# Feed-forward gate product: the second gate goes through a bfloat16 tile in SBUF

## The reference, cut to what matters

```python
def _qdot(x, w, out_dtype=BF16):
    return jnp.dot(x.astype(E4M3), w.astype(E4M3), preferred_element_type=out_dtype)
ff_gate = _qdot(x, w_gating[0])        # 512 -> 2048
gate_value = jax.nn.gelu(ff_gate)
ff1 = _qdot(x, w_gating[1])            # the second gate
activations = gate_value * ff1         # rounded to E4M3 by the next _qdot
outputs = _qdot(activations, w_linear) # 2048 -> 512
```

## Time and profile before

| what | us |
|---|---|
| median of three runs | 1949.02 |
| the profiled execution's own time | 1948.51 |
| its span | 1946.7 |
| TensorE busy in the span | 1867.8 (96%) |
| VectorE busy | 1484.0 (76%) |
| ScalarE busy | 1116.2 (57%) |
| GpSimd busy | 989.0 (51%) |
| first and last product (start) | 1582.5 and 1925.3 |

### The profile page before, as it was taken

The page is one execution under the profiler, slowest core; times in us unless marked ns, Lnnn a source line. Parts: engine busy times, 40 slices in busy tenths (PEclk is TensorE's granted clock), DMA queues, the critical chain, the costliest instruction groups (busy, mean ns, idle before and its releaser), DMA issues.

```text
span 1946.7 us, 31849 instructions
## 1 busy us (share of the span) xinstructions
PE 1867.8 (96%) x11426; PEld 1052.8 (54%) x11460; DVE 1484.0 (76%) x2632; ACT 1116.2 (57%) x2149; POOL 989.0 (51%) x1000
## 2 busy tenths in 40 slices
PE   7899999999999898899999999999999898999998
PEld 4677776777777654344444444444444333444443
DVE  4557676675666657788888888888888548999998
ACT  3345443444444525788888888888888662333331
POOL 3455545555455522344555455444444246666665
PEclk9999999999999878999999999999999999999999
DMA  5665554655555522334433333333333320111111
GB/s 170 177 160 151 134 162 120 175 138 149 147 141 145 140 81 74 110 106 135 135 130 119 114 114 118 122 121 122 121 117 100 116 71 12 44 44 44 46 63 44
DMA packets 149901, 220.58 MB, mean 113 GB/s; under 512 B 41847, under 2 KB 50551, under 8 KB 148999
## 3 DMA queue, kind: packets, MB, share of 16 engines
q1 hardware_dynamic: 140078, 216.96, 37.1%
q10 hardware_dynamic: 9664, 1.58, 0.5%
HBM read 83.95 MB, written 32.02 MB: 60 GB/s over the span
## 4 chain that ended last, share of the span: by engine, by line
PE 73%; DVE 14%; DMA 4%; POOL 3%; ACT 3%; issue 3%; SPq 1%; ACTq 0%; DVEq 0%; POOLq 0%
PE bank L1298 12%; PE bank L1333 11%; PE bank L85 8%; PE bank L1631 7%; PE bank L86 7%; PE bank L87 7%; PE bank L1341 6%; PE bank L1607 4%; PE bank L577 4%; DVE sa_mneg L703 3%; PE bank L631 3%; DVE sa_xnat L717 2%; PE bank L644 2%; DVE ff_prod L1648 1%; DVE ff_hq L1662 1%
## 5 line engine op out<-in xcount | busy, mean ns | idle before, releaser
L1376 DVE TENSOR_REDUCE xa_mneg<-bank 128x1 f32<-128x512 f32 x1024 | 641.9, 681 | 114.7 <-PE bank L1341 109.9
L1196 ACT ACTIVATE xa_prob<-bank 128x512 f32<-128x512 f32 x1024 | 545.1, 609 | 80.6 <-PE bank L1333 77.7
L1341 PE MATMUL bank<-xa_kst,xa_qst 48*128 48x512 f32 x1024 | 383.1, 459 | 10.7 <-DVE xa_mneg L1376 10.6
L1333 PE MATMUL bank<-xa_qst,xa_kst 49*128 49x512 f32 x1024 | 354.2, 441 | 13.8 <-ACT xa_prob L1196 13.5
L468 ACT ACTIVATE sa_prob<-bank 128x512 f32<-128x512 f32 x256 | 152.4, 599 | 335.9 <-PE bank L631 334.9
L1333 PEld LDWEIGHTS bank<-xa_qst,xa_kst 49*128 49x128 f32 x1024 | 163.3, 186 | 295.6 <-ACT xa_prob L1196 241.7
L1298 PE MATMUL bank<-xa_prob,xa_v 128*32 128x512 f32 x2048 | 275.4, 610 | 0.0
L1539 POOL TENSOR_TENSOR ff_total<-ff_prod,ff_mag 128x512 f32<-128x512 bf16 x128 | 195.6, 1528 | 101.4 <-DVE ff_mag L1655 101.3
L703 DVE TENSOR_REDUCE sa_mneg<-bank 128x2 f32<-128x512 f32 x256 | 164.1, 683 | 35.7 <-PE bank L644 35.5
L1341 PEld LDWEIGHTS bank<-xa_kst,xa_qst 48*128 48x128 f32 x1024 | 166.1, 187 | 41.9 <-DVE xa_mneg L1376 34.0
L1583 ACT ACTIVATE ff_gelu<-bank 128x512 bf16<-128x512 f32 x128 | 75.6, 593 | 155.1 <-PE bank L1631 155.1
(11 more groups left out here) (191 smaller groups left out, 3663.5 us busy)
## 6 DMA issues: line engine op xcount, KB each, us to landing
xa_qst<-xa_part_q SPq DMA_DIRECT2D x192, 128.0 KB, 2.7
xa_kst<-xa_part_k SPq DMA_DIRECT2D x192, 128.0 KB, 2.8
sa_qst<-sa_part_qh SPq DMA_DIRECT2D x64, 256.0 KB, 4.1
sa_kst<-sa_part_kh SPq DMA_DIRECT2D x64, 256.0 KB, 5.4
xa_den<-inv SPq DMA_DIRECT2D x64, 256.0 KB
sa_xraw<-xT SPq DMA_DIRECT2D x32, 256.0 KB, 4.3
sa_qst<-sa_part_ql SPq DMA_DIRECT2D x32, 256.0 KB, 4.3
sa_kst<-sa_part_kl SPq DMA_DIRECT2D x32, 256.0 KB, 5.8
```

The costliest lines, as they stand in the source:

```text
L1196: act.activation(prob[place[e]][:, :], banks[eb[e]][:, :], ACT.Exp, scale=X_SCALE)\
L1333: pe.matmul(banks[eb[e]][:, :], kst[u % 3][rows_of, head // 2, t * P:(t + 1) * P], qst[u % 3][rows_of, head // 2, :], start=True, stop=Tru ...
L1341: pe.matmul(banks[mb[m]][:, :], qst[u % 3][rows_of, n // 8, t * P:(t + 1) * P], kst[u % 3][rows_of, n // 8, :], start=True, stop=True).the ...
L1376: dve.tensor_reduce(mneg[:, u % 2, column:column + 1], banks[mb[m]][:, :], AX.X, ALU.max, negate=True).then_inc(s_mfree, 1)
```

## The change

ScalarE copies the second gate of slot n from its PSUM bank into a new bf16 tile `up` in SBUF (three buffers, in the region "parts"), right behind the gelu of the same slot. The copy waits for the matmuls (`s_ub`) and for the product three slots back (`s_prod`). TensorE's reuse of an `ub` bank now waits for the copy (`s_up`), not for the product. VectorE's product waits for the copy and reads `up` and `gelu`, both bf16 in SBUF. The instructions of TensorE, GpSimd and the DMA queues are the same in number and order; ScalarE has 128 more.

```diff
+    up = r.sb("ff_up", [P, 3, COLS], BF16)
...
                 act.activation(gelu[:, n % 4, :], gb[n % 2][:, :], ACT.Gelu_apprx_tanh)\
                    .then_inc(s_gelu, 1)
+                wait.wait_ge(s_ub, n + 1)
+                wait.wait_ge(s_prod, n - 2)
+                act.activation(up[:, n % 3, :], ub[n % 2][:, :], ACT.Copy).then_inc(s_up, 1)
                 if p + 1 < PAIRS and h in turns:
                     round_x(p + 1, turns.index(h))
...
-                    for k, banks, done, free in [(0, gb, s_gb, s_gelu), (1, ub, s_ub, s_prod)]:
+                    for k, banks, done, free in [(0, gb, s_gb, s_gelu), (1, ub, s_ub, s_up)]:
...
             wait.wait_ge(s_gelu, n + 1)
-            wait.wait_ge(s_ub, n + 1)
+            wait.wait_ge(s_up, n + 1)
             wait.wait_ge(s_hs, n - 3)
-            dve.tensor_tensor(prod[:, n % 4, :], ub[n % 2][:, :], gelu[:, n % 4, :], ALU.mult)\
+            dve.tensor_tensor(prod[:, n % 4, :], up[:, n % 3, :], gelu[:, n % 4, :], ALU.mult)\
                .then_inc(s_prod, 1)
```

More of the change, by code:

```diff
@@ L1479, in ffn_phase @@
     s_tb, s_x8, s_xq = s.sem("tb"), s.sem("x8"), s.sem("xq")
-    s_gb, s_ub, s_gelu, s_prod = (s.sem(n) for n in ["gb", "ub", "gelu", "prod"])
+    s_gb, s_ub, s_gelu, s_up, s_prod = (s.sem(n) for n in ["gb", "ub", "gelu", "up", "prod"])
     s_he, s_hm, s_hs, s_hq = (s.sem(n) for n in ["he", "hm", "hs", "hq"])
```

## The result

| | before | after |
|---|---|---|
| median, us | 1949.02 (1944.70 to 1953.71, five runs) | 1965.18 (1963.69 to 1970.16, five runs) |
| ratio after / before | | 1.0089, 95% interval 1.0073 to 1.0106 |
| profiled execution, us | 1948.51 | 1963.69 |
| its span | 1946.7 | 1961.8 |
| start of the first product | 1582.5 | 1578.6 |

The kernel is slower, by 16.2 us of the medians; 1967 was forecast.

The account below looks back on a forecast made before the run. It took VectorE and TensorE to be both at their floor, so longer VectorE slots lengthen the kernel. Terms 7.0, 1.5, 8.9, 0.5 and 0 gave 17.9 us on 1948.5, 1966.4, so a median of 1967; range 1954 to 1985.

Parts of the forecast that it names:

- The product's own length: VectorE's product with both inputs bf16 in SBUF takes 0.42 us, 0.26 less than now.
- The hold and who goes first: In plain slots GpSimd's addition goes first and holds the product: 2.56 us instead of 2.09; other slots 2.89 and 3.16.
- Rival B: The product gets the port ahead of GpSimd's addition and the mask is held instead; 1958 us, chance 0.10.
- Pair 0: Pair 0 and the start of pair 1: 15 intervals at VectorE's pace, 0.47 us longer each, 7.0 us.
- The sets of four in pairs 1 to 7: Sets of four slots grow from 10.80 to 11.17 us, 0.37 each: 1.5 in rest of pair 1, 8.9 in pairs 2 to 7.
- The copies' latency: Where VectorE waits for the gelu, and in the first slot, copies add delay less the product's saving: 0.5 us in all.
- The tail: The 16 slots after the last product, all before the feed-forward, add 0.
- The signs: Plain-slot products about 1.4 us, ending 0.29 after GpSimd's addition, which stays 1.53; TensorE some 96% busy in the steady state.
- A: No hold on the product, or one that costs nothing; plain slots stay 2.09, TensorE's 10.75 stays; 1948 us, chance 0.11.
- C: The hold comes and the product stays at full length; plain slots 2.82, four slots 12.21; 2000 us, chance 0.09.
- D: Faster by over 0.3%: pair 1's two waits, 7.7 us, close as freed banks let TensorE run ahead; 1941, chance 0.03.
- S: Main rival in the experiments: loss comes from ScalarE's 128 copies, the wait for them and later freeing of banks.

Follow-up runs that it names:

- copies_only: Changed kernel with all 128 ScalarE copies kept and waited for, but the product reads the second gate from PSUM; 1951.47 us, ratio to before 1.0001.
- mixed: Changed kernel with copy and SBUF product only in 54 of 128 slots, behind the normalisation or statistics, PSUM in the others; 1946.56 us, ratio to before 0.9986.
- up_f32: Changed kernel with the tile `up` in float32 instead of bf16; 2002.74 us, ratio to before 1.0284.
- order: Changed kernel with VectorE's rounding subtraction moved behind the product, so that the product asks first; 1954.13 us, ratio to before 1.0034.
- the repeats: The changed kernel and the kernel before, each run again unedited; 1968.22 us (ratio 1.011) and 1948.53 us (1.0005).
- memset_after: Changed kernel with a GpSimd memset of 1024 float32 a partition in place of its addition, sum left out; 1941.14 us, ratio 0.9957.

## Why the prediction was right

Where the plain slots grew the kernel grew, and where they did not (copies_only, mixed) it did not: that VectorE's slots bound the kernel was right. But the prediction had both engines at their floor, four slots at 10.80 us, and that is not what the trace says. VectorE's residual additions in slots 23 and 127 lie 26 sets of four slots apart. In the kernel before:
```profile
1648.15 0.69 DVE L1691 TENSOR_TENSOR x_first<-bank,x_first 128x512 f32<-128x512 f32 x1
...
1927.37 0.68 DVE L1691 TENSOR_TENSOR x_first<-bank,x_first 128x512 f32<-128x512 f32 x1
```
In the changed one:
```profile
1651.81 0.69 DVE L1695 TENSOR_TENSOR x_first<-bank,x_first 128x512 f32<-128x512 f32 x1
...
1940.58 0.69 DVE L1695 TENSOR_TENSOR x_first<-bank,x_first 128x512 f32<-128x512 f32 x1
```
That is 10.74 us a set before and 11.11 after. VectorE set the pace before, too, at its own 10.72 to 10.74; only three late sets took 10.80 or more, which is TensorE's pace in mixed. The steps of the prediction, one by one:

- The product's own length: 0.42 forecast, 0.41 measured, and up_f32 shows that the narrow types give it.
- The hold and who goes first: 2.56, 2.89 and 3.16 us forecast for the three kinds of slot, 2.55, 2.88 and 3.13 measured. The order run showed the other half of the mechanism: its slots, worked out by the same rule, came in at 2.42 as expected. (One reading was off by a hair: from 1785.58 to 1786.58 is 1.00 us, not 1.01.) Rival B's case was thus a real one, but it needs another order in the program.
- Pair 0: 7.0 forecast. From the first product to the first residual addition 45.23 us became 52.75, so 7.5.
- The sets of four in pairs 1 to 7: 28 x 0.37 = 10.4 forecast, 9.1 measured. The growth a set came out at 0.37, partly by luck: the set after was forecast 0.06 too long (11.17 for 11.11) and the one before taken 0.06 too long (10.80 for 10.74). And only 26 sets had it: 9.6, less 0.4 because the stretch ends with the last product's start. The first set, over the waits for the cross attention, went from 20.38 to 20.42 us.
- The copies' latency: 0.5 forecast. The two waits went from 3.78 and 3.91 to 4.34 and 4.47, 0.56 longer each, and the product behind each is 0.27 shorter: 0.6 in all, inside the 20.42 us above.
- The tail: nothing forecast, 2.4 us measured (2.1 in the repeats). Some 0.45 of it is the last held product, the rest the clock. The prediction had named a loss of clock as a risk in pair 0. There it came (0.83 between 1600 and 1620 us) and no cost of it can be seen, since VectorE was busy 19.59 of the 20 us; it cost at the end, where TensorE alone sets the pace. This term of the sum failed.
- The sum: 7.5 + 9.1 + 2.4 = 19.0 us, against 17.9. The two measurements of the changed kernel, ratios 1.0089 and 1.011, are 17.3 and 21.4 us and hold it between them. That the first median came within 2 us of 1967 is partly luck, since the stretch ahead of the first product moves by more than that.
- The signs: no copy held VectorE up in the steady state after 1651 us, and the addition stayed at 1.53. TensorE was forecast at some 96% busy there and reads 98%; its few waits are for the subtraction's results and the next input, not for the copy.
- The rivals: A (no hold) came only with GpSimd's addition gone (memset_after), C (full length) only with the wide copy (up_f32). D needed the two waits in pair 1 to close, and they grew. S, which the prediction had only as latency, cost at most 2 us.

The Trainium skill's "SBUF — State Buffer", section "Who interferes with whom", says that a two-input Vector instruction is held by a GpSimd instruction that reads SBUF and not by one that only writes it, and that the issue order decides who waits. The runs agree on this product: 1.38 us beside the addition against 0.43 under a memset, and 0.42 where the product asked first.

## What to carry to other kernels

Before moving an input of a VectorE instruction from PSUM to SBUF, look at what GpSimd does beside it: the instruction alone became 0.27 us cheaper, and a plain slot 0.46 us dearer, because its input in PSUM was what let it pass. Keep the form that GpSimd can't hold where GpSimd works, and take the cheap form where it doesn't: the version with 54 of the copies was the only complete kernel that won. Where an engine feeds TensorE in single steps near the end of a kernel, the waits can also halve the clock of what follows.

## What was not expected of the hardware

- At the end the clock fell to half in the two profiles of the changed kernel, in up_f32 and in order, where the last subtractions come late, and in no profile of the kernel before, of copies_only or of mixed. It costs 1.6 to 1.9 us there (12.96 and 13.24 against 11.35). In pair 0 it fell as well (0.83 in the first profile) and no cost can be seen: the products last 359.4 and 359.5 us in the two profiles.
- GpSimd's addition itself depends on its neighbour: 1.15 us alone, 1.53 behind a subtraction, 1.38 behind the normalisation and 1.26 behind a product of two narrow inputs (order). In the last three it ends 1.00 to 1.02 us after the VectorE instruction ahead of it does.
- How a held instruction ends: 0.29 us after the addition for the product and the normalisation, 0.55 for the subtraction, 0.16 for the mask.
